# Mixing the second half's output projection, residual and norm into the first gate/up chunks of two short feed-forwards

## The reference

```python
# attention, last step                     # feed-forward 1 (sublayer 7 alike, with ternary weights)
out = attn_heads @ w_out                   g = (x @ w_gate) * s_gate
x = layernorm(x + out)                     u = (x @ w_up) * s_up
# layernorm: (x - mean) / sqrt(var + eps)  y = (silu(g) * u) @ w_down * s_down
                                           x = layernorm(x + y)
```

## Time and profile before

| | |
|---|---|
| median of 3 runs | 1169.01 us (1168.03 to 1169.27) |
| the profiled execution: its own time | 1170.22 us |
| its span (first to last instruction) | 1168.5 us |
| mean granted TensorE clock, share of full | 0.896 |
| busy: PE, PEld | 1006.3 us (86%), 570.2 us (49%) |
| busy: DVE, ACT, POOL | 699.4 us (60%), 540.4 us (46%), 331.8 us (28%) |
| first border (sublayer 0 to 1) | about 195 to 229 us of the span |
| second border (sublayer 6 to 7) | about 1086 to 1121 us of the span |

### The profile page before, as it was taken

The page is one execution under the profiler, slowest core; times in us unless marked ns, Lnnn a source line. Parts: engine busy times, 40 slices in busy tenths (PEclk is TensorE's granted clock), DMA queues, the critical chain, the costliest instruction groups (busy, mean ns, idle before and its releaser), DMA issues. The chain is left out here.

```text
span 1168.5 us, 16473 instructions
## 1 busy us (share of the span) xinstructions
PE 1006.3 (86%) x5922; PEld 570.2 (49%) x5922; DVE 699.4 (60%) x1985; ACT 540.4 (46%) x1145; POOL 331.8 (28%) x464
## 2 busy tenths in 40 slices
PE   6999998788699886899999899997757988888785
PEld 2544454674254454437438444444444544445575
DVE  1667773776166794632432567777291688876665
ACT  3566655331768873210110556664304365555422
POOL 3211112331257773000000321112461154532223
PEclk8989998999576786899999889999877899999888
DMA  6000000103000000200000020000000000000000
GB/s 229 1 1 1 1 1 1 50 1 160 1 18 1 1 2 1 106 0 1 1 0 1 1 87 23 1 1 1 1 1 0 1 1 1 1 1 1 1 19 19
DMA packets 4325, 21.61 MB, mean 18 GB/s; under 512 B 377, under 2 KB 1657, under 8 KB 3220
## 3 DMA queue, kind: packets, MB, share of 16 engines
q1 hardware_dynamic: 4244, 20.55, 4.6%
HBM read 19.01 MB, written 1.05 MB: 17 GB/s over the span
## 5 line engine op out<-in xcount | busy, mean ns | idle before, releaser
L897 ACT ACTIVATE PB<-pair 128x1024 f32<-128x1024 f32 (+3 forms) x288 | 223.3, 812 | 135.3 <-PE pair L1621 133.8
L1139 DVE CUSTOM_DVE_ANT_0 junk<-bank,cst 128x128 bf16<-128x128 f32 (+3 forms) x384 | 171.3, 488 | 114.4 <-PE bank L1605 112.0
L730 POOL TENSOR_SCALAR_AFFINE_SELECT PB<-PB 128x256 f32<-128x256 f32 x192 | 79.0, 414 | 327.5 <-ACT PB L897 325.4
L1142 DVE TENSOR_REDUCE pmx<-bank 128x1 f32<-128x512 f32 x192 | 122.8, 685 | 55.9 <-PE bank L1605 54.9
L1605 PE MATMUL bank<-KO_r,QO_r 64*128 64x512 f32 (+3 forms) x576 | 140.2, 417 | 11.1 <-DVE A L1217 3.9
L1637 PE MATMUL pvb<-PB,V 128*32 128x512 f32 (+3 forms) x1152 | 125.3, 507 | 10.8 <-ACT PB L897 8.0
L1605 PEld LDWEIGHTS bank<-KO_r,QO_r 64*128 64x128 f32 x576 | 71.5, 189 | 113.6 <-DVE pmx L1139 38.9
L1617 PE MATMUL pair<-QO_r,KO_r 64*128 64x512 f32 (+3 forms) x576 | 114.4, 388 | 12.7 <-ACT PB L897 11.5
L736 POOL TENSOR_TENSOR parts_r<-y_f,parts_r 128x512 fp32r<-128x512 f32 x24 | 30.8, 1282 | 313.0 <-ACT parts_r L868 313.0
L955 ACT ACTIVATE KO<-pair,nm 128x128 f32<-128x128 f32 x256 | 90.1, 395 | 32.4 <-DVE nm L1288 32.3
L1621 PE MATMUL pair<-ms,sel_r 64*128 64x512 f32 (+3 forms) x576 | 101.1, 343 | 0.0
(11 more groups left out here) (205 smaller groups left out, 1688.7 us busy)
## 6 DMA issues: line engine op xcount, KB each, us to landing
WF<-in_moe_gu SPq DMA_DIRECT2D x1, 3520.0 KB, 10.8
WA<-in_w_att SPq DMA_DIRECT2D x3, 1024.0 KB, 10.7
WF<-in_tern_w SPq DMA_DIRECT2D x1, 3072.0 KB, 9.8
V<-in_moe_d SPq DMA_DIRECT2D x1, 1792.0 KB, 7.5
xT<-in_xT SPq DMA_DIRECT2D x2, 512.0 KB, 5.8
X<-in_x SPq DMA_DIRECT2D x1, 1024.0 KB, 10.6
A<-in_rope SPq DMA_DIRECT2D x1, 1024.0 KB, 4.7
out<-X SPq DMA_DIRECT2D x2, 512.0 KB, 2.9
```

What stands on the lines that cost most here:

```text
L730: pool.affine_select(p2, p2, pattern=[[0, 2], [1, P]], compare_op=ALU.is_ge, fill=0.0, base=0, channel_multiplier=-1).then_inc(causal, 1)
L897: act.activation(pb[:, st % 2, 2 * i:2 * i + 2, 0:n], ps[:, :, 0:n], ACT.Exp, scale=scale)\
L1139: r_done(dve.tensor_tensor_reduce(junk[:, (r_used - 1) % 3, 0:n], ps[:, 0:n], tri[:, HALF - n:HALF], 1.0, LOWEST, ALU.add, ALU.max, accum_ ...
L1142: r_done(dve.tensor_reduce(to, ps[:, 0:n], AX.X, ALU.max))
```

## The change

The second half's end leaves the attention (except in front of the binarised layer) and becomes part of `short_ffn`, in an order written out in the list `FFN_IN`: outT, the four projections, then gate/up of chunk 0, norm part 0, chunk 1, norm part 1, chunk 2, norm part 2, chunk 3, new x, chunk 4, `split_x` of the second half, chunks 5, 6, 7. TensorE takes outT, proj, gu and x1 of that list, DVE takes proj (the residual), norm, gu and split, ACT the copies. So new x comes after four chunks instead of two, DVE does chunks 0, 1 and 2 between the parts of the norm instead of behind it, and `split_x` of the second half comes after chunk 4 instead of chunk 2. `split_x` of the first half moves into the attention's list: it is put ahead of the last but one accT item. No instruction is added or taken away.

```diff
+FFN_IN = [("outT",), ("proj", 0), ("proj", 1), ("proj", 2), ("proj", 3), ("gu", 0), ("norm", 0), ("gu", 1), ("norm", 1),
+          ("gu", 2), ("norm", 2), ("gu", 3), ("x1",), ("gu", 4), ("split",), ("gu", 5), ("gu", 6), ("gu", 7)]
+FFN_OUT, FFN_X1 = (sum(item[0] == "gu" for item in FFN_IN[:FFN_IN.index((name,))]) for name in ("outT", "x1"))
...
+    if SUBLAYERS[s + 1] in (GLU, TERN):
+        plan.insert(max(plan.index(("new",)) + 1, plan.index(("accT",) + STAGES[-2])), ("split",))
...
# ACT
-                copy_transposed(halves_out(s)[1])
+                if SUBLAYERS[s + 1] == BIN:
+                    copy_transposed(halves_out(s)[1])
...
                 for i in range(2 * nf):
+                    if SUBLAYERS[s] != MOE:
+                        for _ in range((FFN_OUT, FFN_X1).count(i)):
+                            copy_transposed(halves_in(s)[1])
...
# DVE, attention
-                if SUBLAYERS[s + 1] in (GLU, TERN):
-                    split_x(s + 1, 0)
-                post(s, 1)
+                    if item[0] == "split":
+                        split_x(s + 1, 0)
+                if SUBLAYERS[s + 1] == BIN:
+                    post(s, 1)
...
# DVE, short_ffn (gated(i) is the body of the old loop over chunks)
+                r_wait()
+                for item in FFN_IN:
+                    if item[0] == "gu":
+                        gated(item[1])
+                    if item[0] == "proj":
+                        residual(s - 1, TH * halves_in(s)[1] + item[1])
+                    if item[0] == "norm":
+                        normalise(s - 1, 1, item[1:])
+                    if item[0] == "split":
+                        split_x(s, 1)
+                post(s, 0)
...
# TensorE, short_ffn
-                        if (half, fc) == (0, LEAD):
-                            new_x(s - 1, halves_in(s)[1])
...
-                gate_up(0)
+                x_split(0)
+                late = halves_in(s)[1]
+                for item in FFN_IN:
+                    if item[0] == "gu":
+                        gate_up(0, item[1])
+                    if item[0] == "outT":
+
+                        pe.wait_ge(r_free, att_done)
+                        transpose_half(A, late)
+                        out_at = e_used
+                    if item[0] == "proj":
+
+                        pe.wait_ge(e_free, out_at)
+                        project_tile(TH * late + item[1], w_att(s - 1, 3 * D, D))
+                    if item[0] == "x1":
+                        new_x(s - 1, late)
                 down(0)
```

More of the change, by code:

```diff
@@ L140, in e_before @@
     return sum(E_USES[k] for k in SUBLAYERS[:s]) - (ND if s else 0)
+FFN_IN = [("outT",), ("proj", 0), ("proj", 1), ("proj", 2), ("proj", 3), ("gu", 0), ("norm", 0), ("gu", 1), ("norm", 1),
+          ("gu", 2), ("norm", 2), ("gu", 3), ("x1",), ("gu", 4), ("split",), ("gu", 5), ("gu", 6), ("gu", 7)]
+FFN_OUT, FFN_X1 = (sum(item[0] == "gu" for item in FFN_IN[:FFN_IN.index((name,))]) for name in ("outT", "x1"))
 def e_chunk(s, i):
-    return e_before(s) + i + 1 + (ND if s and i >= LEAD else 0)
+    if SUBLAYERS[s] == MOE:
+        return e_before(s) + i + 1 + (ND if i >= LEAD else 0)
+    return e_before(s) - ND + i + 1 + (ND if i >= FFN_OUT else 0) + (ND if i >= FFN_X1 else 0)
 OUT_FIRST = {ATT: 1, GLU: 1, WATT: 0, MOE: 0, BIN: 1, TERN: 1}
@@ L978, in ffn @@
                         .then_inc(e_free, 1)
-                    if i == LEAD - 1:
+                    if SUBLAYERS[s] == MOE and i == LEAD - 1:
                         copy_transposed(halves_in(s)[1])
[L981 to L985, removed]
+                        act.wait_ge(logit_max, 1)
+                        act.activation(wm[:, 1, :, :], wm[:, 0, :, :], ACT.Exp).then_inc(logit_exp, 1)
+                        act.wait_ge(ld_sel, 16)
+                        act.activation(selb[:, :], selF[:, :], ACT.Copy).then_inc(cast_ready, 1)
                     if n_hid is not None and fc:
@@ L1374, in split_x @@
                 which = int(s > 1)
-                dve.wait_ge(e_free, e_chunk(s, LEAD) - 1 if k else e_before(s) - ND)
+                dve.wait_ge(e_free, e_chunk(s, FFN_X1) - 1 if k else e_after(s - 1, ("new",)))
                 n = 2 * which + k
@@ L1389, in short_ffn, with gated @@
                 which = int(s > 1)
[L1391 to L1411, removed]
+                def gated(i):
+                    fc = i % NF
+                    n = 2 * NF * which + i
+                    ps = r_slot()
+                    dve.wait_ge(e_free, e_chunk(s, i))
+                    if i >= 2:
+                        dve.wait_ge(h_last, n - 1)
+                    r_done(dve.scalar_tensor_tensor(rest[:, i % 2, :], ps[:, :], up_scale(fc), sg[:, i % 4, :],
+                                                    ALU.mult, ALU.mult))
+                    r_wait()
+                    if i >= 2:
+                        dve.wait_ge(h_typed, n - 1)
+                    dve.tensor_scalar(acc[:, i % 2, :].bitcast(I32), rest[:, i % 2, :].bitcast(I32),
+                                      TOP, None, ALU.bitwise_and).then_inc(h_first, 1)
@@ new lines, in short_ffn @@
+                r_wait()
+                for item in FFN_IN:
[8 more added lines that the diff above has]
+                post(s, 0)
+                for fc in range(NF):
+                    gated(NF + fc)
@@ L1659, in attention @@
                         new_x(s, halves_out(s)[0])
-                last_half_out(s, w_att(s, 3 * D, D), False)
+                if SUBLAYERS[s + 1] == BIN:
+                    last_half_out(s, w_att(s, 3 * D, D), False)
             def windowed(s):
@@ L1799, in short_ffn, with gate_up, x_split @@
                 which = int(s > 1)
-                assert e_used == e_before(s)
+                assert e_used == e_before(s) - ND
+                att_done = r_used
                 pe.wait_ge(*((glu_ready, 2) if s == 1 else (tern_ready, 1)))
-                def gate_up(half):
+                def gate_up(half, fc):
+                    for side in range(2):
+                        ps = e_slot()[:, 0, :] if side == 0 else r_slot()[:, :]
+                        for c in range(ND):
+                            for k in range(2):
+                                last = pe.matmul(ps, gu_r[:, c, side, fc * P:(fc + 1) * P], x_k[half][1][:, k, c, :],
+                                                 start=(c + k == 0), stop=(c + k == 2))
+                        last.then_inc((e_full, r_full)[side], 1)
+                def x_split(half):
                     pe.wait_ge(x_rest, 2 * which + half + 1)
                     pe.wait_ge(x_first, 2 * which + half + 1)
-                    for fc in range(NF):
-                        if (half, fc) == (0, LEAD):
-                            new_x(s - 1, halves_in(s)[1])
[L1810 to L1816, removed]
                 def down(half):
@@ L1830, in down @@
                         last.then_inc(r_full, 1)
-                gate_up(0)
+                x_split(0)
[12 more added lines that the diff above has]
+                        new_x(s - 1, late)
                 down(0)
-                gate_up(1)
+                x_split(1)
+                for fc in range(NF):
+                    gate_up(1, fc)
                 if s < len(SUBLAYERS) - 1:
```

## The result

The changed kernel takes 1185.99 us in the median (1183.31 to 1189.24, 4 runs) against 1168.65 us of before in the same session: a ratio of 1.0148, 95% interval 1.0131 to 1.0164. It is slower by 17.3 us; 13.6 were forecast. The median lies 3.4 us above the forecast of 1182.6 and inside the range of 1173.5 to 1187. Its profiled execution is its second fastest, 1183.61 us with a span of 1181.9 us, so the two traces differ by 13.4 us. A second session gave 1181.47 us (1179.84 to 1184.40, 4 runs) against 1168.96, a ratio of 1.0119 (1.0089 to 1.0149).

The account below looks back on a forecast made before the run. The DVE and POOL chain from the last residual to down was taken to bound both borders. Its +6.3 us (second) and +6.7 (first), plus 0.6 for the early split, made +13.6: 1182.6 us, range 1173.5 to 1187.

Parts of the forecast that it names:

- What bounds the border: At both borders the DVE and POOL chain, 21.69 and 21.71 us, sets the start of down, not TensorE.
- Part 2: Chunks between norm parts: POOL's L722 stalls each part, 3.25 us in all; sum 10.84 us, starting 0.45 later (second border).
- Part 3: New x late at both borders: TensorE idle 5.4 us, half clock on restart; norm to chunk 4 takes 6.1 us.
- Part 4: First half's split inside the attention delays POOL's causal masks: 0.6 us at the first border, 0 at the second.
- Full clock at the restart (1): Same chain, but TensorE keeps full clock at both borders' restarts: +8.5 us, 1177.5 us; chance 0.22.
- norms without stalls (2): L722 does not stall the norm at the borders, TensorE stays at full clock: 1171 us; chance 0.12.
- TensorE as the bound (3): TensorE's chain sets the borders, so filling its hole gains 2 us at each: 1165 us; chance 0.06.
- an order without effect (4): The queue refills and both borders end as before: within 2 us of 1169; chance 0.05.

Follow-up runs that it names:

- experiment 1: Also called norm_first: changed kernel with all three parts of the second half's norm directly behind the residuals, ahead of chunk 0; 1173.18 us, ratio 1.0040.
- experiment 2: Also called pool_short: changed kernel with GpSimd's subtraction of the first half's chunks 0, 1 and 2 cut to 16 of 512 columns; 1174.38 us, ratio 1.0040.
- before_split_last: Also cited as 8: kernel of before with the second half's split behind chunk 7 instead of behind chunk 2; 1167.90 us, ratio 0.9991.
- experiment 3: Also called pe_busy: changed kernel with 22 extra matmuls into a free PSUM bank between chunk 3 and the new x; 1179.45 us, ratio 1.0094.
- split_back_free: Changed kernel with the first half's split at the attention list's end and TensorE's wait for it behind the projections; 1182.13 us against 1181.47.
- before_order_early_split: Changed kernel's code with the order of before in its list, only the first half's split still inside the attention; 1172.82 us, ratio 1.0051.
- warm_down: Kernel of before with extra matmuls into an idle PSUM bank in the four holes ahead of down; 1162.48 us, ratio 0.9950.

## Why the prediction was right, point by point

**What bounds the border.** Right. Down waits for GpSimd in the changed kernel as before (5.25 and 5.27 us), and every edit that shortened the chain on VectorE and GpSimd brought the start of down forward, by 4.0 and 3.7 us (experiment 1), 3.0 and 3.8 (2), 1.9 and 0.7 (8). It is not by as much as was taken out: with the split out of the way TensorE is the next limit (8), and in 1 ACT's queue held up the new x.

**Part 2, the stalls.** Right in kind, place and size. Forecast were 0.93, 1.13 and 1.19 us; measured 0.91, 1.11 and 0.95 at the second border. Residual to norm came out at 11.24 us against 0.45 + 10.84. Experiment 2 shows the cause: same order, short GpSimd operations, 2.9 and 2.8 us less. One reading is loose: the 1.24 us beside 1.28 us that the prediction puts down to L722 are of a row of L736, which has the same form; for L722 itself it is the rows above that show it.

**Part 3, the hole and the clock.** The hole is there (5.24 us at both borders, forecast 5.4) and so is half clock. Its price was set too high: 1.3 and 1.0 us (experiment 3) instead of 2.6. I had let all of the transposes, gate and up of chunk 4 run at half clock; in the trace the clock is back with up 4, which takes 1.08 us from 219.96 and 1.09 us from 1121.44 on. How long it stays away is not fixed: the second session's trace has 5.67 us at its second border. There, and at the first border of split_back_free (5.68), the clock is 0.50 over the whole step, so 2.1 us is what half clock costs at most in these traces, and 2.6 was too much even for that. The forecast for residual to down was too long by 1.6 us at each border: 1.3 and 1.6 for this, 0.3 and 0.1 for part 2. Down itself, which the prediction let vary by 1.7 us with the clock, came to the next norm 0.9 us later and 0.2 earlier.

**Part 4, the early split.** The mechanism was right, the size three times too small. In the changed kernel the four masks take 2.43 instead of 1.82 us, the 0.6 that I took. I had it as half of a bound, with no row for it, so the hit was luck; the trace gives the reason: the first mask starts at 183.70, when the split's two-input L1395 (183.11 to 184.34) has 0.64 us left.

```profile
183.70 2.43 POOL L739 TENSOR_SCALAR_AFFINE_SELECT PB<-PB 128x256 f32<-128x256 f32 x4 [3.81 <-ACT PB L906]
...
185.56 0.92 PE L1661 MATMUL pvb<-PB,V 128*32 128x256 f32 x8 [0.94 <-POOL PB L739]
```

But TensorE waits 0.94 us for them, where it had no such wait before, and from 186.2 to 189.6 has half clock, so the delay grows: from norm part 2 in that attention to A are 20.7 to 20.9 us in all six traces of kernels with the early split, and 19.0 in all seven of kernels without it. That is 1.7 to 1.9 us. The granted clock from 184 to 190 of the span is 0.72 to 0.83 in the six and 1.00 in the seven. What I missed is that a delay of 0.6 us can cost a stretch at half clock. That the early split brings this cost is shown by the six and the seven; that it goes by way of the masks is read from the rows. At the second border the masks take 1.81 us, and there is no cost, as forecast: the same stretch is 20.5 to 21.0 us in kernels of either kind. The Trainium skill's rule ("SBUF — State Buffer", "SBUF: two separate sides") covers the masks too, and the trace agrees (2.43 against 1.82 us); what it would have made of the sum, 0.7 us more than I took, is also short of the 1.9 that the clock made of it.

**What none of the parts had.** In the changed kernel's two traces and in pool_short's the outT and projections of the first border run at full clock (1.00 from 199 to 204), 6.95 us instead of 9.55: a gain of 2.6. I gave that stretch as unchanged. The early half clock alone is not what spares it: norm_first, pe_busy and before_order_early_split have the early split and the early half clock too, and 10.5 us there. What decides between the two stays open. The 0.6 us more at the second border are no mark of the change either: 9.90 and 9.91 us stand there in before_split_last and warm_down, which leave that stretch as it was.

**The sum.** From residual to down the loss is 5.1 and 4.7 us: 2.9 and 2.8 for the stalls (experiment 2), 1.3 and 1.0 for half clock (experiment 3), and 0.9 at both for the order itself, as pool_short with full clock at its second border has it too (22.62 against 21.78). Trace against trace, the whole is: 1.9 for the split, 5.1 and 4.7 from residual to down, -2.6 and +0.6 from A to residual, +0.9 and -0.2 from down to the norm: 10.4 us. The remaining 3.0 is one step in the windowed sublayer, from the norm of the half that feeds it to its first half's norm, 166.8 instead of 163.4 us, less 0.4 elsewhere. That 0.4 is again a balance: 1.5 us less ahead of the first attention's norm, where nothing was changed, and 1.4 more behind the second border, where the last down takes 10.61 instead of 9.21 us with more of it at half clock. The code of the windowed step is the same, and the value is no mark of the change: it is 163.6 in its second trace, 167.0 in before_split_last and 160.4 in before_order_early_split. With it goes the clock in a part of that step:

```profile
350.00:400.00 50.00, 46.32 (x356) 0.66 0.01 2
```

is the changed kernel (granted clock 0.66); before and the changed kernel's second trace have 0.76 in the same 50 us. Over all ten traces of the first two sessions the step takes 166.8 to 167.0 us where these 50 us have 0.66 or 0.67, 163.4 to 163.6 where they have 0.76 to 0.80, and 160.4 in the one with 0.90, whatever the kernel. So the 13.4 us of the traces hit my 13.6 in part by chance: the chain was 3.3 us shorter than forecast, the split 1.3 dearer, the stretch from A to residual 2.0 shorter, down 0.7 longer, and 3.4 us are such luck. The median of the first session lies another 2.4 us above its profiled execution, that of the second 1.1. The slower runs (1188.37 and 1189.24) have a mean granted clock of 0.882 against 0.886 and 0.889 in the other two; which stretches these are stays open, as no trace of them is there.

**The rivals.** Full clock at the restart (1) failed in both traces; norms without stalls (2) is what experiment 2 makes of the kernel, 1174 us where 1171 was said; TensorE as the bound (3) is refuted by the hole ahead of down, which grew; an order without effect (4) is refuted by the time and by every stretch above.

## What to carry to other kernels

Filling an engine's idle time is worth nothing while another engine's chain sets the end: mark that chain first, then ask of each move whether it makes that chain shorter. Small VectorE instructions on SBUF that are put next to a long two-input GpSimd operation risk its whole length (here a tensor_scalar and a tensor_tensor of four columns did, at 0.17 us each when alone), so keep them in a block on one side of it. When the bound engine waits for others, look at what it needs latest (here a split wanted only after down) and at the clock that TensorE loses in its holes: these two gave 14.9 us, where the reordering cost 17.3.

## What the runs showed of the hardware

- Half clock follows short waits too: 0.94 us of waiting at 185.56, in a stretch with other short gaps, was followed by it. The length of one hole doesn't tell it: ahead of the second border's new x, 2.01 us were followed by full clock before and by half clock in warm_down, and behind 2.32 and 2.31 us in pool_short the first border had half clock and the second full.
- Plain extra matmuls on data at hand held the clock: behind 0.9 to 5 us of them the transposes took 1.09 to 1.10 us and down ran to the next norm in 11.8 to 12.2 us at both borders; warm_down met half clock behind the second border's new x (transposes of 1.97 us), where there were none.
- GpSimd is delayed by VectorE as well as the other way round: six of the eight L731 at the second border take 1.26 to 1.29 us, the one that meets L1102 1.37, and the one that meets the split's first instruction 1.67.
- Not every pair meets like this. The aggregations of the norm took 0.37 us beside L731, as when alone, and in the trace before the change the norm's instructions of four columns, with two SBUF inputs, took 0.16 us beside a one-input GpSimd operation of 2.00 us (L742, from 850.25 on).
